# Two node blocks a slot, and twelve passes a layer, for a graph layer's one-hot gathers on TensorE

## The chip, the core and the metric

The kernel runs on one core of a Trainium2 chip. The metric is device time in microseconds (us). The engines are called by their names here and by their short names in the profile: TensorE (PE, its weight loads PEld), VectorE (DVE), ScalarE (ACT), GpSimd (POOL), SyncE (SP). ACTq and SPq are rows of DMAs that ScalarE and SyncE issue.

## The reference, cut to what matters

Two layers of a graph transformer over N = 3125 nodes of D = 128 features and E = 103125 edges that are sorted by their destination; H = 8 heads of 16.

```python
h = relu(layernorm(x0))                          # x0 is the input
for l in range(2):
    xn = layernorm(h) * g1 + b1
    xp = xn + xn @ Wpos + bpos + deg * Wdeg + bdeg   # deg: normalised degree of a node
    q, k, v = (xp @ Wq + bq), (xp @ Wk + bk), (xp @ Wv + bv)
    att   = clip(sum_per_head(q[dst] * k[src]) / 4, -50, 50)
    ex    = exp(att)                             # the softmax's shift cancels
    aggr  = segment_sum(v[src] * ex, dst) / segment_sum(ex, dst)
    h = h + aggr @ Wo + bo
    h = h + gelu(layernorm(h) @ W1 + b1) @ W2 + b2
return x0 + h
```

The edges are the given ones and one self loop per node. What costs time is k[src] and v[src]: a row of 256 floats (1 KB) per edge, from a table of 3200 rows.

## The kernel before, in words

**Tiles and groups.** The edges are 806 tiles of 128 (one edge per partition), handled in groups of 4 tiles: 202 groups a layer, 404 in all (`GROUPS`). The nodes are 25 blocks of 128 (`BLOCKS`). The first 6 groups of a layer are "seam" groups, whose tiles reach over two node blocks and cost two one-hots instead of one. Node blocks are sorted by how soon their edges end, in 9 chunks of 2 or 3 blocks (`CHUNKS`); when all edges of a chunk are summed, its dense work (output projection, norms, feed-forward, the next layer's q, k, v) is laid over the following 21 slots. From the slot of group 31 on some chunk is always in that state.

**A slot** is one turn of the unrolled loop that each engine runs; the engines are tied by semaphores only. In slot n:
- GpSimd (L908 to L920) runs ahead by up to `RING` = 8 groups. It issues one indirect DMA per tile, which gathers 128 rows of 1 KB from the table in HBM into `kvr`.
- TensorE runs `edge_q(n+1)` (L1190: query rows per edge as one-hot times q, 8 matmul records), `edge_sum(n-1)` (L1202: one-hot times messages, 8 records), one `pick` if one is due (L1214), then dense parts. `edge_q(n+1)` waits for VectorE's product of group n, since bank 2 is a single buffer, and for ScalarE's `onehotT`.
- VectorE runs `edge_iteration(n)` (L1891): the product (L1854), the messages of group n-1 (L1878), the sum per head (L1859), clip and guard (L1864, L1869), four additions to `agg` (L1889), the one-hot of group n+2 (L1840); then dense parts.
- ScalarE runs the two exponentials of group n (L1456, L1459), `edge_spread(n+2)` (L1414, L1418, which makes `onehotT`), one `pick_hots` if one is due (L1420), then dense parts.
- SyncE loads `relT` for ScalarE, row by row the one tile in each of 11 groups (`ROW_GROUPS`) that GpSimd does not gather, and stores tables and outputs.

**Picks.** In 7 groups a layer (`PICK_GROUPS` = 36, 63, ... 198) two of the four tiles (`PICKS` = 2) are not gathered by GpSimd but by TensorE, as a product of a one-hot with the whole table. One pass goes over the 25 node blocks, one a slot. For a block, ScalarE issues the DMA of its 128 KB of the table into `pick_kv` (L1433), and makes the one-hot for 256 edges in two operations, |src - node| and relu(1 - ...), each 128x256 (L1438, L1440). TensorE multiplies (L1224, four records a block, 128x256) and accumulates in `picked` (bank 7). Two buffers of `pick_kv` and `pick_hot` alternate. `pick_keep` (L1445) copies the result into `kvr`. So GpSimd issues 806 - 11 - 14 = 781 gathers a layer.

**Prologue.** Blocks are ranked, degrees counted, and the first table is computed. SyncE's order is: bias rows (L695), 14 copies of source rows into `pick_table` (L701), `rel_table` and `relT` (L704, L716), the first `pick_src` (L725), 11 copies into `row_src` (L730), the 13 stores of the first table (L739), the copies of q and x into rank order (L746, L751). GpSimd's first gather waits for the 13 stores.

The lines that say it:

```python
PICK_GROUPS = [36 + 27 * i for i in range(7)]                       # L176
PICK_AHEAD = BLOCKS + 3
        return gathers(n) - by_rows(n) - PICKS * by_pick(n)         # pool_gathers
                if n >= RING:
                    pool.wait_ge(s_msg, n - RING + 1)               # L917
                if n:
                    pe.wait_ge(s_prod, n)                           # L1195, edge_q
                pe.wait_ge(s_msg, n + 1)                            # L1204, edge_sum
```

## Time and profile before

| | |
|---|---|
| runs | 2130.23 us median of three (2128.7 to 2131.04) |
| the profiled execution | 2131.35 us; its span 2129.6 us |
| busy share of the span | PE 73%, PEld 62%, DVE 80%, ACT 58%, POOL 71% |
| granted TensorE clock, mean | 0.917 of full speed |
| chain that ended last | POOL 56%, issue 21%, DVE 8%, DMA 5%, PE 5% |
| costliest groups, us busy | POOL gathers L920 1480; PE L1198 529, L1211 518, L1224 385; DVE L1889 471, L1840 283 |
| DMA | 334 MB in all, mean 157 GB/s; from ScalarE's queue (q10) 47.6 MB |

A busy share is a mean over the whole span. The times of matmul records overlap, since they are pipelined: what one step costs is read from start to start in the timeline. The same holds of VectorE's and ScalarE's rows, where one instruction's record overlaps the next by some 0.1 us. "issue" is time in which an engine waited for nothing that the profile shows.

### The profile page before, as it was taken

The page shows a single profiled execution, that of the slowest core. Times are in us where ns is not written, and L with a number is a line of the kernel's source. Part 1 is how long each engine was busy: PE and PEld are TensorE (multiplying, and loading weights), DVE is VectorE, ACT ScalarE, POOL GpSimd, SP SyncE. Part 2 cuts the span into 40 slices and gives each one's busy share as a digit, 9 for nine tenths or more (in the row PEclk, how much of TensorE's full clock was granted, in tenths as well). Part 3 has the DMA queues.
Part 4 walks back from the last instruction along what each step waited for, and adds up shares of the span by engine and source line. Part 5 has one row for each costly group of instructions (what it writes and reads, how often), then busy time and mean ns, then how long its engine had stood idle before and what let it go on. Part 6 is the DMA issues. An engine that isn't in the chain of part 4 may idle for free.

```text
span 2129.6 us, 45086 instructions
## 1 busy us (share of the span) xinstructions
PE 1561.9 (73%) x9627; PEld 1317.3 (62%) x9627; DVE 1694.2 (80%) x4743; ACT 1232.0 (58%) x2893; POOL 1520.4 (71%) x1620
## 2 busy tenths in 40 slices
PE   4867678787777687777876777767677777777776
PEld 3656566666666566666656666656566666666565
DVE  8759788888888888888877778777787877787775
ACT  8325566575757565665654446556564656456564
POOL 7077777777777777777727777777777777777773
PEclk9979989899999999999988889999998999899998
DMA  2365555555555555555525555555555555555551
GB/s 89 110 190 164 180 175 169 177 174 170 157 167 162 173 160 167 161 163 170 156 71 164 164 163 160 161 158 169 166 157 161 164 169 152 167 163 166 155 159 51
DMA packets 179620, 334.20 MB, mean 157 GB/s; under 512 B 39730, under 2 KB 114684, under 8 KB 179356
## 3 DMA queue, kind: packets, MB, share of 16 engines
q0 software_dynamic: 75424, 205.75, 34.3%
q1 hardware_dynamic: 51660, 77.96, 11.1%
q10 hardware_dynamic: 52272, 47.60, 7.5%
q8 instruction: 88, 1.44, 0.3%
q14 instruction: 176, 1.44, 0.2%
HBM read 319.48 MB, written 8.39 MB: 154 GB/s over the span
## 4 chain that ended last, share of the span: by engine, by line
POOL 56%; issue 21%; DVE 8%; DMA 5%; PE 5%; ACT 3%; SPq 1%; DVEq 0%; ACTq 0%; POOLq 0%
POOL kvr L920 56%; DMA kvr<-kv_table,srcidx 5%; DVE agg L1889 2%; DVE kvr L1495 2%; PE bank L1198 1%; PE bank L1211 1%; DVE msg L1878 1%; ACT L1373 1%; DVE prod L1854 1%; ACT apart L1414 0%; DVE onehot L1840 0%; ACT L1456 0%; PE bank L1155 0%; ACT onehotT L1418 0%; SPq L730 0%
## 5 line engine op out<-in xcount | busy, mean ns | idle before, releaser
L920 POOL DMA_INDIRECT kvr<-kv_table,srcidx x1562 | 1480.1, 948 | 541.7 <-issue 465.7
L1198 PE MATMUL bank<-q,onehotT 128*128 x3320 | 528.7, 309 | 503.8 <-DVE prod L1854 300.7
L1198 PEld LDWEIGHTS bank<-q,onehotT 128*128 128x128 f32 x3320 | 454.6, 212 | 637.7 <-issue 633.0
L1456 ACT ACTIVATE bank<-attc 128x32 f32<-128x32 f32 x404 | 81.2, 201 | 794.0 <-DVE attc L1869 787.5
L1211 PE MATMUL bank<-msg,onehot 128*128 128x136 f32 x3320 | 517.7, 306 | 0.6 <-DVE msg L1878 0.6
L1889 DVE TENSOR_TENSOR agg<-agg,bank 128x136 f32 x1624 | 471.4, 290 | 55.6 <-PE bank L1211 32.1
L1854 DVE TENSOR_TENSOR prod<-kvr,bank 128x512 f32<-128x512 f32 (+1 forms) x404 | 273.5, 677 | 279.2 <-DMA kvr<-kv_table,srcidx 244.2
L1211 PEld LDWEIGHTS bank<-msg,onehot 128*128 128x128 f32 x3320 | 479.1, 216 | 2.3 <-DVE msg L1878 2.2
L1224 PE MATMUL bank<-pick_kv,pick_hot 128*128 128x256 f32 x1400 | 384.9, 399 | 13.8 <-DMA pick_kv<-kv_table 12.6
L1414 ACT ACTIVATE apart<-relT,minus_p 128x512 bf16<-128x512 bf16 x416 | 293.9, 706 | 5.3 <-DMA relT<-rel_table 4.9
L1878 DVE TENSOR_TENSOR msg<-kvr,bank 128x512 f32<-128x512 f32 (+1 forms) x404 | 271.6, 672 | 25.2 <-ACT bank L1456 24.9
L1224 PEld LDWEIGHTS bank<-pick_kv,pick_hot 128*128 128x128 f32 x1400 | 256.9, 203 | 43.7 <-issue 20.5
L1840 DVE TENSOR_TENSOR onehot<-bank,rel 128x512 f32<-128x512 f32 x416 | 283.1, 683 | 0.2
L1859 DVE TENSOR_REDUCE att<-prod 128x32 f32<-128x512 f32 x404 | 273.7, 677 | 0.1
L1418 ACT ACTIVATE onehotT<-apart 128x512 f32<-128x512 bf16 x416 | 261.9, 630 | 13.1
L1438 ACT ACTIVATE pick_apart<-pick_src,minus_node 128x256 bf16<-128x256 f32 x350 | 172.4, 493 | 0.2
L1440 ACT ACTIVATE pick_hot<-pick_apart 128x256 f32<-128x256 bf16 x350 | 145.9, 417 | 11.1
L1459 ACT ACTIVATE msg<-attc 128x32 f32<-128x32 f32 x404 | 85.9, 213 | 0.0
L1864 DVE TENSOR_SCALAR attc<-att 128x32 f32<-128x32 f32 x404 | 79.0, 196 | 0.1
L1869 DVE SCALAR_TENSOR_TENSOR attc<-att,attc 128x32 f32<-128x32 f32 x404 | 75.3, 187 | 0.0
L1456 ACT ACT_TABLE_LOAD x54 | 69.3, 1283 | 1.0
L1155 PE MATMUL bank<-w,hT 128*128 128x128 f32 x400 | 57.9, 288 | 0.0
(223 smaller groups left out, 973.3 us busy)
## 6 DMA issues: line engine op xcount, KB each, us to landing
relT<-rel_table SPq DMA_DIRECT2D x104, 512.0 KB
kv_rows<-kv_table SPq DMA_DIRECT2D x2816, 1.0 KB
pick_kv<-kv_table ACTq DMA_DIRECT2D x350, 128.0 KB
kvr<-kv_table,srcidx POOLq DMA_INDIRECT x1562
loop_kv<-kv_table SPq DMA_DIRECT2D x25, 128.0 KB
kv_table<-qkv SPq DMA_DIRECT2D x25, 128.0 KB
kv_table<-onehot SPq DMA_DIRECT2D x8, 256.0 KB, 2.7
w<-weights SPq DMA_DIRECT2D x2, 840.0 KB, 7.3
```

Source lines behind the costliest of these rows:

```text
L920: pool.indirect_dma_start(kvr[:, n % RING, j, :], None, kv_table[l], bass.IndirectOffsetOnAxis(ap=srcidx[:, step:step + 1], axis=0)).then_ ...
L1198: mm = pe.matmul(bank[2][:, j * D:(j + 1) * D], onehotT[:, m % OHT, j, :], q[:, bass.ds(ranks[j + h], 1), :].rearrange("p a c -> p (a c)") ...
L1211: mm = pe.matmul(sum_ps(n, k), onehot[:, m % OH, j, :], msg[:, n % 2, j, :], start=(m, j) == of[0], stop=(m, j) == of[-1])
L1224: mm = pe.matmul(picked[:, j * KV:(j + 1) * KV], pick_hot[:, m % 2, j * P:(j + 1) * P], pick_kv[:, m % 2, :], start=b == 0 and j == 0, sto ...
L1414: act.activation(apart[:], relT[:, m // BODY % REL_BUFS, r, :], ACT.Abs, bias=minus_p[:]).then_inc(s_apart, 1)
L1418: act.activation(onehotT[:, m % OHT, :, :].rearrange("p j e -> p (j e)"), apart[:], ACT.Relu, bias=1.0, scale=-1.0).then_inc(s_ohT, 1)
L1438: act.activation(pick_apart[:], pick_src[:], ACT.Abs, bias=minus_node[:, b:b + 1]).then_inc(s_pick_apart, 1)
L1840: dve.tensor_tensor(onehot[:, m % OH, :, :], iota_ps.unsqueeze(1).broadcast_to([P, G, P]), rel[:, row:row + G].unsqueeze(2).broadcast_to([ ...
L1854: dve.tensor_tensor(prod[:, 0:t, :], kvr[:, n % RING, 0:t, 0:D], bank[2][:, 0:t * D].rearrange("p (j c) -> p j c", c=D), ALU.mult).then_in ...
L1859: dve.tensor_reduce(att[:, n % 2, 0:t * H], prod[:, 0:t, :].rearrange("p j (h d) -> p (j h) d", d=HD), AX, ALU.add).then_inc(s_att, 1)
L1878: dve.tensor_tensor(by_head(msg[:, n % 2, 0:t, 0:D]), by_head(kvr[:, n % RING, 0:t, D:KV]), ex[:, 0:t * H].rearrange("p (j h) -> p j h", h ...
L1889: dve.tensor_tensor(target, target, sum_ps(n, j), ALU.add).then_inc(s_agg, 1)
```

## The change

- `PICK_GROUPS` has 12 groups a layer (24, 39, ... 189) in place of 7. GpSimd issues 806 - 11 - 24 = 771 gathers a layer.
- A pass takes 13 slots (`PICK_STEPS`): 12 with two node blocks and one with the last. One DMA brings both blocks (256 KB), eight matmul records multiply them.
- ScalarE makes the one-hot of the first block of a slot, with its two operations as before. VectorE makes that of the second, at the end of its `edge_iteration`, with one `tensor_scalar` (is_equal, 128x256 float32, compared with a per-partition scalar of `node`).
- The buffers of the picks move into `x_nat` for layer 0 and into `loops` for layer 1. The first `pick_src` of each layer is loaded by SyncE, behind the x copies and behind the last use of `loops`. The loads of x0 also wait for the last pick of layer 0.
- In the prologue the copies into `pick_table` (now 24) and into `row_src` (11) are issued by ScalarE, behind the square root of the degrees, and no longer by SyncE ahead of the table's stores. SyncE waits for both before it copies q.
- `ROW_GROUPS` begins with 23 in place of 24.

```diff
-ROW_GROUPS = [24 + 17 * i for i in range(11)]
+ROW_GROUPS = [23] + [41 + 17 * i for i in range(10)]
-PICK_GROUPS = [36 + 27 * i for i in range(7)]
+PICK_GROUPS = [24 + 15 * i for i in range(12)]
 PICKS = 2
-PICK_AHEAD = BLOCKS + 3
+PICK_STEPS = -(-BLOCKS // 2)
+PICK_AHEAD = PICK_STEPS + 3
...
@@ SyncE
-            sp.wait_ge(s_rows_f, 2)
-            for i, g in enumerate(PICK_GROUPS):
...
-            sp.wait_ge(s_pick_table, 16 * PICKS * len(PICK_GROUPS))
-            sp.dma_start(pick_src[:], pick_table[0:1, :].broadcast_to([P, PICKS * P])).then_inc(s_pick_src, 16)
-
-            sp.wait_ge(s_rows, 16 * 2 * SC)
-            for i, g in enumerate(ROW_GROUPS):
...
             sp.wait_ge(s_row_src, 16 * len(ROW_GROUPS))
+            sp.wait_ge(s_pick_table, 16 * PICKS * len(PICK_GROUPS))
@@ TensorE, pick(k, t)
+                pe.wait_ge(s_pick_kv[m % 2], 16 * (m // 2 + 1))
+                for h in range(min(2, BLOCKS - 2 * t)):
+                    b = 2 * t + h
+                    if h == 0:
+                        pe.wait_ge(s_pick_hot_act, k * PICK_STEPS + t + 1)
+                    else:
+                        pe.wait_ge(s_pick_hot_dve, k * (BLOCKS // 2) + t + 1)
+                    for j in range(PICKS):
+                        mm = pe.matmul(picked[:, j * KV:(j + 1) * KV], pick_hot[l][:, m % 2, h, j * P:(j + 1) * P], pick_kv[l][:, m % 2, h, :], start=b == 0 and j == 0, stop=b == BLOCKS - 1 and j == PICKS - 1)
@@ ScalarE
             act.activation(degstd[:], degsum_ps, ACT.Sqrt, scale=1.0 / (N - 1)).then_inc(s_degstd, 1)
+            act.wait_ge(s_rows_f, 2)
+            for i, g in enumerate(PICK_GROUPS):
+                for j in range(PICKS):
...
+                    act.dma_start(pick_table[i:i + 1, j * P:(j + 1) * P], step_src_f[row:row + 1, c * P:(c + 1) * P]).then_inc(s_pick_table, 16)
+            act.wait_ge(s_rows, 16 * 2 * SC)
+            for i, g in enumerate(ROW_GROUPS):
...
+                act.dma_start(row_src[i % ROW_PARTS:i % ROW_PARTS + 1, i // ROW_PARTS, :], step_src[row:row + 1, c * P:(c + 1) * P]).then_inc(s_row_src, 16)
@@ ScalarE, pick_hots(k, t)
+                act.dma_start(pick_kv[l][:, m % 2, 0:nb, :], kv_table[l].rearrange("(b p) c -> p b c", p=P)[:, b:b + nb, :]).then_inc(s_pick_kv[m % 2], 16)
@@ VectorE
+            def pick_hots(k, t):
+
+                l, m, b = k // len(PICK_GROUPS), k * PICK_STEPS + t, 2 * t + 1
+                if t == 0:
+                    dve.wait_ge(*pick_src_loaded(k))
+                if m >= 2:
+                    dve.wait_ge(s_picked, m - 1)
+                dve.tensor_scalar(pick_hot[l][:, m % 2, 1, :], pick_src[l], node[:, b:b + 1], None, ALU.is_equal).then_inc(s_pick_hot_dve, 1)
...
                         edge_iteration(n)
+                        k, t = pick_at(n)
+                        if k is not None and 2 * t + 1 < BLOCKS:
+                            pick_hots(k, t)
```

## Rows read from the trace of the kernel before

**Rows 1.** GpSimd's gathers by line, the first gather of layer 0, GpSimd's wait for the ring.

```profile
L920 POOL DMA_INDIRECT kvr<-kv_table,srcidx x1562 | 1480.1, 948 | 541.7 <-issue 465.7 <-DMA kv_table<-qkv 38.6 <-DMA kv_table<-xn 27.7
103.70 0.99 POOL kvr L920
POOL kvr L920 <- DVE msg L1878: 9.8, 32, 0.3
```

**Rows 2.** Windows: us, busy us (instructions) by engine, granted clock, DMA share, GB/s.

```profile
200.00:600.00 400.00, 309.05 (x1850) 260.61 (x1851) 347.42 (x1001) 245.57 (x562) 303.06 (x319) 0.92 0.58 172
600.00:1050.00 450.00, 336.00 (x2054) 282.69 (x2053) 370.16 (x1068) 277.74 (x618) 340.26 (x361) 0.93 0.56 164
1200.00:2050.00 850.00, 623.05 (x3793) 529.66 (x3792) 660.82 (x1875) 491.43 (x1123) 643.04 (x680) 0.93 0.55 162
```

**Rows 3.** VectorE's waits for gathers: in 120:1090, in 300:500, in 1120:2098.

```profile
DVE prod L1854 <- DMA kvr<-kv_table,srcidx: 79.2, 62, 3.4
...
DVE prod L1854 <- DMA kvr<-kv_table,srcidx: 4.6, 7, 1.4
...
DVE prod L1854 <- DMA kvr<-kv_table,srcidx: 165.0, 116, 4.4
```

**Rows 4.** Timeline of VectorE: first and last product of layer 0.

```profile
127.11 0.69 DVE L1854 TENSOR_TENSOR prod<-kvr,bank 128x512 f32<-128x512 f32 x1 [7.99 <-issue]
...
1092.80 0.42 DVE L1854 TENSOR_TENSOR prod<-kvr,bank 128x256 f32<-128x256 f32 x1
```

**Rows 5.** Timelines: two neighbouring products on VectorE; one slot of TensorE.

```profile
460.77 0.68 DVE L1854 TENSOR_TENSOR prod<-kvr,bank 128x512 f32<-128x512 f32 x1
...
464.31 0.68 DVE L1854 TENSOR_TENSOR prod<-kvr,bank 128x512 f32<-128x512 f32 x1
...
462.65 1.15 PE L1198 MATMUL bank<-q,onehotT 128*128 x8 [0.48 <-ACT onehotT L1418]
...
464.56 1.03 PE L1224 MATMUL bank<-pick_kv,pick_hot 128*128 128x256 f32 x4
465.52 0.33 PE L935 MATMUL bank<-bias,ones 3*128 3x384 bf16 x1
```

**Rows 6.** The chain of work: one slot of TensorE at the lower clock.

```profile
393.53 2.07 PE bank L1198 x8
395.60 1.81 PE bank L1211 x8
397.41 1.71 PE bank L1224 x4
```

**Rows 7.** VectorE operations near the new one: timelines, then two lines' durations.

```profile
82.20 0.87 DVE L1654 SCALAR_TENSOR_TENSOR onehot<-u_deg,deg,bank 128x256 f32<-128x256 f32 x2
...
455.86 0.86 DVE L1701 TENSOR_SCALAR xn<-x,mv,rstd 128x128 f32<-128x128 f32 x3
...
L1701 DVE TENSOR_SCALAR xn<-x,mv,rstd x75: 329/345/557, 298.2 to 2117.6; 128x128 f32<-128x128 f32 x75
...
L1584 DVE TENSOR_SCALAR w<-w x2: 220/249/278, 23.3 to 23.9; 128x128 f32<-128x128 f32 x2
```

**Rows 8.** DMA queue q10, that of ScalarE; TensorE's wait for the picks' loads.

```profile
q10 hardware_dynamic: 52272, 47.60, 7.5%
...
PE bank L1224 <- DMA pick_kv<-kv_table: 12.6, 21, 2.1
```

**Rows 9.** Timelines of the prologue: SyncE's DMA issues, VectorE's last product for the table.

```profile
73.53 4.24 SPq L701 DMA_DIRECT2D pick_table<-onehotT  x14
...
82.88 8.23 SPq L730 DMA_DIRECT2D row_src<-q  x11
...
98.56 0.71 SPq L739 DMA_DIRECT2D kv_table<-xn  x1
100.51 19.12 SPq L746 DMA_DIRECT2D q<-qkv  x25
...
94.27 0.48 DVE L1654 SCALAR_TENSOR_TENSOR xn<-u_deg,deg,bank 128x256 f32<-128x256 f32 x1
```

More of the change, by code:

```diff
@@ L387, in build @@
         kv_rows = sb("kv_rows", [P, 2, KV])
-        pick_src = sb("pick_src", [P, PICKS * P])
-        pick_kv = sb("pick_kv", [P, 2, KV])
-        pick_apart = sb("pick_apart", [P, PICKS * P], BF16)
-        pick_hot = sb("pick_hot", [P, 2, PICKS * P])
+        node = sb("node", [P, BLOCKS])
         minus_node = sb("minus_node", [P, BLOCKS])
@@ L450, in build @@
         x0 = x_nat
+        spare = [t[:].rearrange("p b c -> p (b c)") for t in (x_nat, loops)]
+        pick_src = [t[:, 0:PICKS * P] for t in spare]
+        pick_kv = [t[:, 2 * P:2 * P + 4 * KV].rearrange("p (u h c) -> p u h c", u=2, h=2) for t in spare]
+        pick_hot = [t[:, 2 * P + 4 * KV:2 * P + 8 * KV].rearrange("p (u h c) -> p u h c", u=2, h=2) for t in spare]
+        pick_apart = [t[:, 2 * P + 8 * KV:3 * P + 8 * KV].bitcast(BF16) for t in spare]
         spare = q[:].rearrange("p b c -> p (b c)")
@@ L572, in build @@
         s_pick_apart = sem("s_pick_apart")
-        s_pick_hot = sem("s_pick_hot")
+        s_pick_hot_act = sem("s_pick_hot_act")
+        s_pick_hot_dve = sem("s_pick_hot_dve")
+        s_pick_first = sem("s_pick_first")
         s_picked = sem("s_picked")
@@ L695, in _ @@
                 sp.dma_start(bias3[k:k + 1, :, :], bias_parts[k * L * RC:(k + 1) * L * RC, :].rearrange("c (a e) -> c a e", a=1)).then_inc(s_bias3, 16)
-            sp.wait_ge(s_rows_f, 2)
-            for i, g in enumerate(PICK_GROUPS):
-                for j in range(PICKS):
-                    c, row = divmod(row_of(g, at_begin=True) + G - PICKS + j, P)
-                    sp.dma_start(pick_table[i:i + 1, j * P:(j + 1) * P], step_src_f[row:row + 1, c * P:(c + 1) * P]).then_inc(s_pick_table, 16)
             sp.wait_ge(s_rel_bf, 1)
@@ L722, in _ @@
                 rel_rows(body)
-            sp.wait_ge(s_pick_table, 16 * PICKS * len(PICK_GROUPS))
-            sp.dma_start(pick_src[:], pick_table[0:1, :].broadcast_to([P, PICKS * P])).then_inc(s_pick_src, 16)
-            sp.wait_ge(s_rows, 16 * 2 * SC)
-            for i, g in enumerate(ROW_GROUPS):
-                c, row = divmod(row_of(g, at_begin=True) + ROW_TILE, P)
-                sp.dma_start(row_src[i % ROW_PARTS:i % ROW_PARTS + 1, i // ROW_PARTS, :], step_src[row:row + 1, c * P:(c + 1) * P]).then_inc(s_row_src, 16)
             table = kv_table[0].rearrange("(b p) c -> p b c", p=P)
@@ L751, in _, with first_pick_src @@
                     sp.dma_start(x[:, bass.ds(r, 1), :], x_nat[:, b0 + j:b0 + j + 1, :]).then_inc(s_x_ranked, 16)
+            def first_pick_src(l):
+                if l == 0:
+                    sp.wait_ge(s_x_ranked, 16 * BLOCKS)
+                else:
+                    sp.wait_ge(s_looped, NCH)
+                sp.dma_start(pick_src[l], pick_table[0:1, :].broadcast_to([P, PICKS * P])).then_inc(s_pick_first, 16)
+            first_pick_src(0)
             def load_loops(c):
@@ L1212, in edge_sum, with pick @@
                 mm.then_inc(s_agg_ps, 1)
-            def pick(k, b):
-                m = k * BLOCKS + b
-                if b == 0 and k:
+            def pick(k, t):
+                l, m = k // len(PICK_GROUPS), k * PICK_STEPS + t
+                if t == 0 and k:
                     pe.wait_ge(s_pick_kept, k)
-                if b == 0 and k % len(PICK_GROUPS) == 0:
-                    pe.wait_ge(s_agg, sums_by(k // len(PICK_GROUPS) * GROUPS + SEAM_GROUPS))
-                pe.wait_ge(s_pick_hot, m + 1)
+                if t == 0 and k % len(PICK_GROUPS) == 0:
+                    pe.wait_ge(s_agg, sums_by(l * GROUPS + SEAM_GROUPS))
                 pe.wait_ge(s_pick_kv[m % 2], 16 * (m // 2 + 1))
-                for j in range(PICKS):
-                    mm = pe.matmul(picked[:, j * KV:(j + 1) * KV], pick_hot[:, m % 2, j * P:(j + 1) * P], pick_kv[:, m % 2, :], start=b == 0 and j == 0, stop=b == BLOCKS - 1 and j == PICKS - 1)
+                for h in range(min(2, BLOCKS - 2 * t)):
+                    b = 2 * t + h
+                    if h == 0:
+                        pe.wait_ge(s_pick_hot_act, k * PICK_STEPS + t + 1)
+                    else:
+                        pe.wait_ge(s_pick_hot_dve, k * (BLOCKS // 2) + t + 1)
+                    for j in range(PICKS):
+                        mm = pe.matmul(picked[:, j * KV:(j + 1) * KV], pick_hot[l][:, m % 2, h, j * P:(j + 1) * P], pick_kv[l][:, m % 2, h, :], start=b == 0 and j == 0, stop=b == BLOCKS - 1 and j == PICKS - 1)
                 mm.then_inc(s_picked, 1)
```

41 lines of the change are left out of this document (23 added, 18 removed).

## The prediction, made blind

> **What bounds the kernel.** I read the chain of waits first: more than three quarters of it is GpSimd's gathers and the "issue" time between them. The groups by line give the step: 1480.1 us busy and 465.7 us of issue in 1562 gathers, 1.25 us each, and in all only 9.8 us of waiting for a free place in the ring [rows 1]. So GpSimd walks at a constant pace through both layers, 781 x 1.25 = 976 us in each, or 4.83 us a group (976 / 202), and the other engines only have to keep up. How nearly they do is the question of this case. The windows show VectorE busy 87% in the first part of layer 0, 82% in its second part, 78% in layer 1, and TensorE 77%, 75% and 73% [rows 2]. VectorE's waits for gathers are its true spare time: 165 us in layer 1, 79.2 in layer 0, and only 4.6 us between 300 and 500 [rows 3]. There the chain of VectorE, TensorE and ScalarE already fills GpSimd's pace.
>
> **Fewer gathers.** 20 x 1.25 = 25.0 us off GpSimd, 12.5 a layer, if it stays the one that sets the pace. Its pace becomes 771 x 1.25 / 202 = 4.77 us a group.
>
> **The prologue.** SyncE spends 4.24 us on 14 copies into pick_table and 8.23 us on 11 into row_src ahead of the table's stores. The last store goes out at 98.56, though VectorE finished the data at 94.27 + 0.48 = 94.75 [rows 9]. With the copies gone the stores follow VectorE, whose products come 0.8 us apart or slower, and SyncE's issue of one takes 0.7. So the last leaves at about 94.85 and GpSimd begins 3.7 us earlier than 103.70 [rows 1, 9]. ScalarE's new queue: 24 issues of 0.30 and 11 of 0.75, 15.5 us, taken at SyncE's price since no row has them from ScalarE. It was idle there until its first edge spreads, and their results are needed only when q is in place. But SyncE's copies of q, which began at 100.51 [rows 9], wait for those row copies. They could begin when the stores are out, near 95.6, or as late as before: 0 to 4.9 us are won. I take 1.6, nearer the lower end, because ScalarE can start its 15.5 us only after the degrees' root. So the first product, at 127.11 [rows 4], comes at 125.5. Should the 35 issues cost double, it comes 15.5 us later than that, and this falls on layer 0.
>
> **VectorE's new operation.** 12 x 12 x 2 = 288 of them, 144 a layer. No row has this form. The nearest is a scalar_tensor_tensor of 256 columns with a per-partition scalar: two take 0.87 us and one 0.48, so a step of 0.39 [rows 7, 9]. The tensor_scalar of 128 columns with such scalars has a step of (0.86 - 0.345) / 2 = 0.26 [rows 7]. A product of 512 columns takes 0.68 and one of 256 takes 0.42 [rows 4, 5], 0.13 for 128 columns, and 0.26 + 0.13 is the same 0.39. Bounds: 0.33 if the added columns went at double rate, 0.48 if it never overlapped its neighbour, 9 us less or 12 more in a layer. I take 0.395: 56.9 us a layer. A bare VectorE slot grows from 464.31 - 460.77 = 3.54 us [rows 5] to 3.94.
>
> **TensorE's second block.** One block costs 465.52 - 464.56 = 0.96 us, and the slot without dense parts 465.52 - 462.65 = 2.87; with two blocks it is 3.83 [rows 5]. At the lower clock (1.2 of 2.4 GHz) the same slot takes 2.07 + 1.81 + 1.71 = 5.6 [rows 6] and would take 7.3. On average TensorE was busy 309 us in 400, 3.73 a group of 4.83 [rows 2]. Blocks per group rise from 25/27 to 25/15, which adds 0.74 x 0.96 = 0.71: 4.44 of 4.77, 93%. VectorE comes to 347.4 / 400 x 4.83 + 0.395 x 12/15 = 4.51, 95%. Two engines at such shares, tied one slot apart by edge_q's wait for the product, hold each other up: the dense slots of TensorE (feed-forward) are others than those of VectorE (norms, scores). What this costs VectorE per hot slot is in no row. From below it is 0: TensorE's longer stretches of work leave fewer gaps, and the clock, which the windows show at 0.92 to 0.93 with gaps, may be granted in full more often. From above it is 0.96 - 0.395 = 0.56, TensorE's added work pacing every slot. I take 0.15, near the lower end, since a bare slot of 3.83 still fits under 3.94: 21.6 us a layer.
>
> **ScalarE and the queues.** ScalarE makes 312 one-hots in place of 350 and ten more copies of `picked`: no more work than before, and it is not on the path. The loads of picks carry 600 blocks in place of 350. That queue's 7.5% of sixteen engines is 160 us, 0.46 for one load of 128 KB, so 0.91 for a double one, and TensorE was already late for 21 of 350 by 12.6 us [rows 8]. I count nothing extra: edge_q of the next slot has about a microsecond before VectorE needs it. If that cover is gone, 0.46 in each of 288 slots is inside the 0.56 above. The other added waits (s_pick_hot_dve before the next pick_src, VectorE's wait for `picked` of two steps before, SyncE's for x and `loops`) all ask for things finished a slot or more earlier, and what stands behind them on SyncE has slots in hand.
>
> **The sum.** Layer 0, between first and last product: 1092.80 - 127.11 = 965.7 [rows 4], less 79.2 of waiting for gathers, is 886.5 us that the chain of engines itself needs. With the change: 886.5 + 56.9 + 21.6 = 965.0, and the last product comes at 125.5 + 965.0 = 1090.5, 2.3 us earlier than before. GpSimd alone would allow 1092.8 - 3.7 - 12.5 = 1076.6. So I expect layer 0 to be set by the VectorE and TensorE chain, with GpSimd waiting for its ring, and most of its 12.5 us lost. Layer 1 has 165 us of spare against 56.9 + 21.6 + 12.5, so it keeps 12.5 us. Together 14.8 us: 2131.35 - 14.8 = 2116.5 for a profiled execution. That one stands 1.1 us over the median of the three runs, so the median would be 2115.4. I say 2115.
>
> **Rivals.**
> - *Everything is kept* (chance 0.27). If the hold-up per hot slot stays below (1076.6 - 125.5 - 886.5 - 56.9) / 144 = 0.05 us, GpSimd paces both layers. The ring of 8 groups, some 38 us, would bridge the tight stretch from 300 to 500. Time: 2130.2 - 3.7 - 25.0 = 2101.5. For it: the clock could rise. Against it: the two shares of 93 and 95%.
> - *TensorE becomes the bound* (0.15). From a hold-up of (14.8 + 21.6) / 144 = 0.25 us per hot slot on, the kernel is slower than before. At 0.40 layer 0 ends 33.7 us after the old time (36.0 more than at 0.15, less 2.3), layer 1 still keeps its 12.5, since 56.9 + 57.6 + 12.5 is under 165: 2151. For it: one slot at the lower clock needs 7.3 us, over one and a half of GpSimd's groups, and double loads may come late. Against it: such stretches should get rarer.
> - *VectorE's new operation stops GpSimd* (0.04). Then each of 288 gathers that it meets is held for up to its own 0.39 us, 112 us: 2130 - 15 + 112 = 2227. The rows speak against it: the tensor_scalar on L1701 lies between gathers too, takes 329 ns at least and 345 in the middle [rows 7], and GpSimd's step stays 1.25 [rows 1]. The one on L1584, with an immediate as its scalar, takes 220 to 249, less by about what 64 to 128 columns cost, so only the form with an immediate seems to run at double rate, and the new one has a per-partition scalar. The Trainium skill has the rule that speaks for it: VectorE: DVE Perf Modes, "The perf-mode tier table", gives fp32 tensor_scalar double rate from SBUF, and SBUF — State Buffer, "Who interferes with whom", says that an operation in such a two-port mode locks GpSimd out for its whole length.
> - *The prologue gives nothing and the rest little* (0.07): the 35 issues are slow on ScalarE, layer 0 starts late, and the time comes within a few microseconds of before, 2128.
>
> My own case, the partial gain, has 0.47. The range of 8 in 10 goes from 2100, just under the full gain, to 2132, a hold-up of 0.26 us. Faster or slower counts from 0.2%, 4.3 us, which is about what a measurement of this kernel can tell from no change. Faster 0.75: my case and the full gain, with a little of the last rival. Same 0.09: most of the last rival and the near edge of the second. Slower 0.16: the rest.
>
> **What would show it.** In the profile after: 1542 gathers at 1.25 us, the first near 100 us. GpSimd's wait for the messages (its ring), 9.8 us before, grows to some tens of us, all in layer 0; in layer 1 it stays small. VectorE's wait for gathers in layer 0 shrinks from 79 us to near 10, that in layer 1 to about 80. L1224's successor has 2400 records. The new VectorE group has 288 instructions with durations of 0.4 to 0.5 us. TensorE is busy near 85% with a granted clock over 0.93. If GpSimd's ring wait stays under 10 us, the full gain is right. If VectorE waits for TensorE (agg for bank, prod for bank) by more than 60 us, the second rival is. If gathers have a step over 1.25, the third.

## The result, and the profile after

The changed kernel takes 2100.49 us (median of four runs, 2098.28 to 2102.06); the kernel before, on the same chip, 2130.64 (2128.7 to 2131.25). The ratio is 0.9856, with a 95% interval of 0.9844 to 0.9867: 30.1 us, or 1.4%, faster. The forecast was 2115. The case that came true is the first rival, everything kept, at 2101.5; that it lies within 1 us is in part luck (see below). The profiled execution took 2100.35 us with a span of 2098.6, and the differences below are of its span, 31.0 us.

The page of the kernel after: the first line, GpSimd's gathers by line, the chain of waits, ScalarE's DMA queue.

```profile
PE 1715.5 (82%) x10627; PEld 1468.3 (70%) x10627; DVE 1770.0 (84%) x5031; ACT 1206.7 (58%) x2827; POOL 1506.9 (72%) x1601
...
L925 POOL DMA_INDIRECT kvr<-kv_table,srcidx x1542 | 1466.4, 951 | 526.4 <-issue 459.3
...
POOL 34%; issue 19%; DVE 19%; PE 12%; DMA 8%; ACT 6%; DVEq 1%; SPq 0%; ACTq 0%
...
q10 hardware_dynamic: 85360, 81.57, 12.8%
```

1542 gathers, 20 fewer, at the old step: (1466.4 + 459.3) / 1542 = 1.249 us. TensorE went from 73 to 82% of the span and VectorE from 80 to 84%. The chain that ended last runs less through GpSimd (34%, before 56%) and more through VectorE and TensorE, but that chain is one path traced back and not a measure of who holds whom. The wait for the ring is.

Waits of the kernel after: GpSimd's and TensorE's in the whole span, then VectorE's in 120:1085 (layer 0) and in 1100:2078 (layer 1). Columns: us in total, times, longest.

```profile
POOL kvr L925 <- DVE msg L1898: 10.1, 33, 0.3
...
PE bank L1234 <- DMA x_nat<-kv_table: 27.6, 39, 2.4
...
PE bank L1234 <- DMA loops<-kv_table: 25.7, 39, 3.4
...
DVE prod L1874 <- DMA kvr<-kv_table,srcidx: 17.9, 11, 4.7
DVE agg L1909 <- PE bank L1216: 16.5, 35, 2.0
DVE prod L1874 <- PE bank L1203: 16.5, 17, 8.0
DVE msg L1898 <- ACT bank L1476: 15.9, 13, 2.1
...
DVE prod L1874 <- DMA kvr<-kv_table,srcidx: 115.7, 89, 4.5
```

GpSimd waits 10.1 us for its ring, as before (9.8, [rows 1]): nothing holds it, in either layer. TensorE waits 53.3 us for the picks' loads where it waited 12.6 [rows 8], and that does not reach GpSimd's pace either.

Windows of the kernel after, the same stretches as [rows 2], and the columns of them.

```profile
200.00:600.00 400.00, 343.28 (x2120) 295.18 (x2119) 368.72 (x1081) 243.72 (x556) 302.92 (x319) 0.97 0.64 193
600.00:1050.00 450.00, 381.87 (x2359) 326.58 (x2358) 400.42 (x1171) 276.47 (x614) 341.01 (x358) 0.97 0.61 183
...
1200.00:2050.00 850.00, 702.99 (x4330) 607.55 (x4328) 708.66 (x2046) 487.83 (x1111) 643.48 (x678) 0.96 0.60 181
```

In the first window VectorE is 92% busy and TensorE 86%, and GpSimd still issues its gathers at the old pace. The granted clock rose from 0.92 and 0.93 to 0.97 and 0.96: TensorE, fuller now, ran more of its time at the upper of its two levels, 2.4 GHz.

Timelines of the kernel after: the first gather and the last of layer 0, the first of layer 1; the first and last product of layer 0; ScalarE's new DMA issues and SyncE's copies of q; one slot of TensorE with two node blocks.

```profile
100.31 1.00 POOL L925 DMA_INDIRECT kvr<-kv_table,srcidx  x1 [23.29 <-DMA kv_table<-xn]
1068.53 0.95 POOL L925 DMA_INDIRECT kvr<-kv_table,srcidx  x1 [0.30 <-issue]
1103.18 0.94 POOL L925 DMA_INDIRECT kvr<-kv_table,srcidx  x1 [33.70 <-DMA kv_table<-qkv]
...
127.77 0.69 DVE L1874 TENSOR_TENSOR prod<-kvr,bank 128x512 f32<-128x512 f32 x1 [8.04 <-PE bank L1203]
...
1075.59 0.42 DVE L1874 TENSOR_TENSOR prod<-kvr,bank 128x256 f32<-128x256 f32 x1
...
82.72 0.17 ACT L1344 ACTIVATE degstd<-bank 128x1 f32<-128x1 f32 x1 [0.93 <-PE bank L1080]
82.73 7.58 ACTq L1349 DMA_DIRECT2D pick_table<-onehotT  x24
90.36 7.21 ACTq L1353 DMA_DIRECT2D row_src<-q  x11
...
100.47 19.90 SPq L738 DMA_DIRECT2D q<-qkv  x25
...
455.27 1.15 PE L1203 MATMUL bank<-q,onehotT 128*128 x8 [0.89 <-ACT onehotT L1437]
456.26 1.09 PE L1216 MATMUL bank<-msg,onehot 128*128 128x136 f32 x8
457.38 1.97 PE L1234 MATMUL bank<-x_nat 128*128 128x256 f32 x8
```

With the same marks read from both traces (before: first gathers at 103.70 and 1120.46, last ones at 1080.94 and 2096.85; after: last one at 2068.87), the 31.0 us divide so:

| stretch | before | after | gain |
|---|---|---|---|
| to the first gather | 103.7 | 100.3 | 3.4 |
| gathers of layer 0, first to last | 977.2 | 968.2 | 9.0 |
| last gather to last product, layer 0 | 11.9 | 7.1 | 4.8 |
| last product to the first gather of layer 1 | 27.7 | 27.6 | 0.1 |
| gathers of layer 1 | 976.4 | 965.7 | 10.7 |
| last gather to last product, layer 1 | 7.4 | 4.5 | 3.0 |
| last product to the end | 25.3 | 25.2 | 0.1 |

(The rounded gains add to 31.1.) So both layers kept their gain, and each also ended with VectorE closer behind GpSimd. I had forecast nothing of the kind.

### The profile page after: what moved, and what is told of

Read it like the earlier page. It is cut to its first block, busy times and chain, and to the rows that moved or that the text cites. A ratio compares the mean times of both kernels' runs of the same rounds, so it can differ in the third digit from the quotient of the medians.

```text
span 2098.6 us, 47279 instructions
## 1 busy us (share of the span) xinstructions
PE 1715.5 (82%) x10627; PEld 1468.3 (70%) x10627; DVE 1770.0 (84%) x5031; ACT 1206.7 (58%) x2827; POOL 1506.9 (72%) x1601
## 3 DMA queue, kind: packets, MB, share of 16 engines
q1 hardware_dynamic: 51424, 78.08, 11.1%
## 4 chain that ended last, share of the span: by engine, by line
POOL 34%; issue 19%; DVE 19%; PE 12%; DMA 8%; ACT 6%; DVEq 1%; SPq 0%; ACTq 0%
POOL kvr L925 34%; DVE agg L1909 6%; DMA kvr<-kv_table,srcidx 4%; DMA x_nat<-kv_table 3%; PE bank L1203 3%; PE bank L1234 3%; PE bank L1216 3%; DVE kvr L1515 2%; DVE onehot L1860 2%; DVE prod L1874 1%; ACT apart L1433 1%; DVE msg L1898 1%; DVEq L672 1%; ACT L1476 1%; PE bank L1160 1%
## 5 line engine op out<-in xcount | busy, mean ns | idle before, releaser
L925 POOL DMA_INDIRECT kvr<-kv_table,srcidx x1542 | 1466.4, 951 | 526.4 <-issue 459.3
L1203 PE MATMUL bank<-q,onehotT 128*128 x3320 | 494.4, 296 | 274.2 <-DVE prod L1874 134.0
L1909 DVE TENSOR_TENSOR agg<-agg,bank 128x136 f32 x1624 | 472.2, 291 | 50.8 <-PE bank L1216 26.6
L1216 PE MATMUL bank<-msg,onehot 128*128 128x136 f32 x3320 | 486.6, 293 | 1.0 <-DVE msg L1898 0.8
L1216 PEld LDWEIGHTS bank<-msg,onehot 128*128 128x128 f32 x3320 | 448.0, 204 | 3.0 <-DVE msg L1898 2.8
L1234 PE MATMUL bank<-loops 128*128 128x256 f32 x1200 | 296.4, 390 | 29.2 <-DMA loops<-kv_table 25.7
L1234 PE MATMUL bank<-x_nat 128*128 128x256 f32 x1200 | 294.1, 387 | 31.6 <-DMA x_nat<-kv_table 27.6
L1433 ACT ACTIVATE apart<-relT,minus_p 128x512 bf16<-128x512 bf16 x416 | 294.0, 707 | 15.2 <-issue 14.8
L1234 PEld LDWEIGHTS bank<-loops 128*128 128x128 f32 x1200 | 219.2, 193 | 67.1 <-DMA loops<-kv_table 36.7
L1234 PEld LDWEIGHTS bank<-x_nat 128*128 128x128 f32 x1200 | 217.1, 191 | 68.6 <-DMA x_nat<-kv_table 39.3
L1479 ACT ACTIVATE msg<-attc 128x32 f32<-128x32 f32 x404 | 85.9, 213 | 0.0
L1458 ACT ACTIVATE loops<-loops,minus_node 128x256 bf16<-128x256 f32 x156 | 76.9, 493 | 2.7 <-PE bank L1234 2.6
L1458 ACT ACTIVATE x_nat<-x_nat,minus_node 128x256 bf16<-128x256 f32 x156 | 76.8, 492 | 0.0
```

Source lines behind the costliest of these rows:

```text
L925: pool.indirect_dma_start(kvr[:, n % RING, j, :], None, kv_table[l], bass.IndirectOffsetOnAxis(ap=srcidx[:, step:step + 1], axis=0)).then_ ...
L1203: mm = pe.matmul(bank[2][:, j * D:(j + 1) * D], onehotT[:, m % OHT, j, :], q[:, bass.ds(ranks[j + h], 1), :].rearrange("p a c -> p (a c)") ...
L1216: mm = pe.matmul(sum_ps(n, k), onehot[:, m % OH, j, :], msg[:, n % 2, j, :], start=(m, j) == of[0], stop=(m, j) == of[-1])
L1234: mm = pe.matmul(picked[:, j * KV:(j + 1) * KV], pick_hot[l][:, m % 2, h, j * P:(j + 1) * P], pick_kv[l][:, m % 2, h, :], start=b == 0 and ...
L1433: act.activation(apart[:], relT[:, m // BODY % REL_BUFS, r, :], ACT.Abs, bias=minus_p[:]).then_inc(s_apart, 1)
L1458: act.activation(pick_apart[l], pick_src[l], ACT.Abs, bias=minus_node[:, b:b + 1]).then_inc(s_pick_apart, 1)
```

## The experiments

Two accounts stood against each other first. **A**: GpSimd's pace sets both layers, so the gain is that of the gathers, and the engines behind it have room. **B**: much of the gain comes from elsewhere than the gathers (the clock, the rearranged work). Where an expectation names another, it says what that holds. Ratios are to the kernel before, run on the same chip.

**Seven passes.** The changed kernel with the old number of passes, at groups 24 to 186.

```diff
-PICK_GROUPS = [24 + 15 * i for i in range(12)]
+PICK_GROUPS = [24 + 27 * i for i in range(7)]
```

> Two blocks a slot, one-hots and prologue as in the changed kernel, but 7 passes a layer: 781 gathers a layer in place of 771. Theory A (GpSimd's gathers pace both layers, the rest only follows): 20 gathers more at 1.25 us, so 2100.5 + 25 = about 2125, and VectorE's wait for gathers in layer 0 grows from 18 us to over 60. Theory B (the gain came from the slots being packed otherwise and from the fuller clock): less than 12 us over the changed kernel, under 2112.

2121.21 us, ratio 0.9951 (0.9934 to 0.9969). The five passes a layer are worth 20.7 us. That is more than B allows (under 12), and near A's 25; VectorE's wait for gathers in layer 0 is 61.9 us, as A said. In the two profiled executions the gathers of the layers take 24.1 us more with seven passes than with twelve. This kernel's share of the gain, some 9 us, comes without one gather less. 3.6 us are the earlier first gather (100.08), and 7.6 the ends of the layers: the last product trails the last gather by 8.3 and 3.4 us, against 11.9 and 7.4 before. (Its gathers give 4.4 us back, and the way to layer 1's first gather 2.7, in a profiled execution of 2127.07 us, 5.9 over its median.) Both kernels, this one and the kernel before, have seven passes; the last one is now that of group 186 instead of 198 and takes 13 slots instead of 25. Its mean granted clock is 0.888, the lowest of all profiled executions, so the clock is not what pays.

**The prologue undone.** The 35 copies go back to SyncE, ahead of the stores.

```diff
@@ SyncE, ahead of the stores of the first table
+            sp.wait_ge(s_rows_f, 2)
...
+                    sp.dma_start(pick_table[i:i + 1, j * P:(j + 1) * P], step_src_f[row:row + 1, c * P:(c + 1) * P]).then_inc(s_pick_table, 16)
...
+                sp.dma_start(row_src[i % ROW_PARTS:i % ROW_PARTS + 1, i // ROW_PARTS, :], step_src[row:row + 1, c * P:(c + 1) * P]).then_inc(s_row_src, 16)
@@ ScalarE
-            act.wait_ge(s_rows_f, 2)
...
-                    act.dma_start(pick_table[i:i + 1, j * P:(j + 1) * P], step_src_f[row:row + 1, c * P:(c + 1) * P]).then_inc(s_pick_table, 16)
...
-                act.dma_start(row_src[i % ROW_PARTS:i % ROW_PARTS + 1, i // ROW_PARTS, :], step_src[row:row + 1, c * P:(c + 1) * P]).then_inc(s_row_src, 16)
```

> The changed kernel with the copies into pick_table and row_src back on SyncE's queue, ahead of the table's stores. Theory A (GpSimd paces from its first gather on): that gather moves from 100.3 to some us later (with 24 copies in place of 14, to about 106), and the time with it, 2104 to 2107. Theory B (layer 0 is paced by the chain of VectorE and TensorE, whose first product came no earlier in the changed kernel than before): no more than 1 us, unless that first product moves too.

2107.26 us, ratio 0.9888 (0.9873 to 0.9903): 6.8 us lost. Its first gather goes out at 106.91, 6.6 us after the changed kernel's.

```profile
106.91 0.99 POOL L935 DMA_INDIRECT kvr<-kv_table,srcidx  x1 [30.91 <-DMA kv_table<-xn]
```

So 6.6 us at the first gather are 6.8 at the end, about as A said. The first product moved too, but by 4.2 us only (to 131.97), so a layer paced from there would have lost less. It is more than 3.4 because twelve passes need 24 copies where seven needed 14.

**ScalarE makes both one-hots.** VectorE has no new operation.

```diff
@@ ScalarE, pick_hots(k, t)
-                act.activation(pick_apart[l], pick_src[l], ACT.Abs, bias=minus_node[:, b:b + 1]).then_inc(s_pick_apart, 1)
...
-                act.activation(pick_hot[l][:, m % 2, 0, :], pick_apart[l], ACT.Relu, bias=1.0, scale=-1.0).then_inc(s_pick_hot_act, 1)
+                for h in range(nb):
...
+                    act.activation(pick_apart[l], pick_src[l], ACT.Abs, bias=minus_node[:, b + h:b + h + 1]).then_inc(s_pick_apart, 1)
...
+                    act.activation(pick_hot[l][:, m % 2, h, :], pick_apart[l], ACT.Relu, bias=1.0, scale=-1.0).then_inc(s_pick_hot_act, 1)
@@ VectorE
-                        if k is not None and 2 * t + 1 < BLOCKS:
+                        if False:
```

> ScalarE makes both one-hots of a slot, VectorE none. Theory A (VectorE's 144 operations a layer fit into spare time and GpSimd paces): the time stays within 5 us below that of the changed kernel, 2096 to 2101; VectorE's wait for gathers in layer 0 grows from 18 us by about 37. The long gathers (over 970 ns) fall from 73 to near the 18 of the kernel before. Theory C (ScalarE has no room: onehotT comes late): slower, over 2105, with TensorE's wait for onehotT well over 129 us.

2096.6 us, ratio 0.984 (0.9823 to 0.9857): 3.9 us less than the changed kernel. That is inside A's figure, but the intervals of the two ratios overlap, and 2.3 us of it lie ahead of the first gather (98.0 against 100.31), in a stretch that the edit does not touch: kernels with the same prologue have their first gather anywhere from 98.0 to 100.3. Another 2.6 lie in the two layers' gathers. The waits are the finding. VectorE's in 120:1085:

```profile
DVE prod L1873 <- PE bank L1203: 29.3, 22, 8.4
DVE agg L1908 <- PE bank L1216: 27.1, 66, 2.5
DVE msg L1897 <- ACT bank L1475: 22.9, 12, 3.1
DVE rstd L1716 <- ACT std L1258: 17.3, 12, 1.6
...
DVE prod L1873 <- DMA kvr<-kv_table,srcidx: 4.0, 3, 3.3
```

VectorE was relieved of 37 us in layer 0, and its wait for gathers did not grow by that, as A had said: it fell from 17.9 to 4.0, and the waits for TensorE and ScalarE took its place. Under whose name spare time stands depends on which of several inputs comes last. This run does not show that VectorE's being faster is the whole reason, since ScalarE has 132 us more work in each layer and is later for the others: the wait for `std` (17.3) was 0.2 in the changed kernel, and TensorE's for `onehotT` rose from 129.1 to 147.3 in the whole span. The one-hot made twice, below, is the cleaner test.

**The one-hot as tensor_tensor.** The same comparison against a broadcast column.

```diff
-                dve.tensor_scalar(pick_hot[l][:, m % 2, 1, :], pick_src[l], node[:, b:b + 1], None, ALU.is_equal).then_inc(s_pick_hot_dve, 1)
+                dve.tensor_tensor(pick_hot[l][:, m % 2, 1, :], pick_src[l], node[:, b:b + 1].broadcast_to([P, PICKS * P]), ALU.is_equal).then_inc(s_pick_hot_dve, 1)
```

> VectorE's one-hot as tensor_tensor with the node number broadcast, which has two inputs and cannot run at double rate. If the new operation runs at double rate now (step 0.26 us) and stops GpSimd's gathers at times, then the step grows to about 0.33 to 0.40, the long gathers (over 970 ns) fall from 73 to about 20, and the time stays within 3 us of 2100.5, since 10 to 20 us more of VectorE fit into layer 0's spare 18. If the long gathers come from the heavier DMA traffic instead, about 73 stay.

2105.02 us, ratio 0.9877 (0.9855 to 0.9898), 4.5 us slower; the intervals of this ratio and the changed kernel's overlap. The new operation by line (in the changed kernel its mean record is 366 ns):

```profile
L1942 DVE TENSOR_TENSOR x_nat<-x_nat,node 128x256 f32<-128x256 f32 x144 | 60.1, 417 | 4.1 <-PE bank L1234 4.1
```

Start to start it takes 0.33 us, as expected. I had thought that with this form fewer gathers would be stretched, about 20. More were: 90 gathers take over 970 ns, against 73 in the changed kernel, and 69 of the 90 overlap one of these operations in time. The gathers of the two layers take 4.9 us longer (969.8 and 969.0), which is where the time went. The last sections come back to this.

**The one-hot made twice.** VectorE does each new operation a second time into unused space: 144 more operations and 37 us more work a layer.

```diff
+                dve.tensor_scalar(pick_more[l][:, 0, :], pick_src[l], node[:, b:b + 1], None, ALU.is_equal)
                 dve.tensor_scalar(pick_hot[l][:, m % 2, 1, :], pick_src[l], node[:, b:b + 1], None, ALU.is_equal).then_inc(s_pick_hot_dve, 1)
```

> The changed kernel with VectorE's one-hot made twice (the second copy into a place nobody reads): 144 operations a layer more, 0.26 us each, 37 us. Theory A (the chain of VectorE and TensorE had 18 us of spare left in layer 0 and 116 in layer 1, so layer 0 is near its edge): layer 0 grows by about 37 - 18 = 19 us, layer 1 not, 2115 to 2125, and GpSimd starts to wait for its ring. Theory D (there is far more slack than the waits show): under 2106.

2102.65 us, ratio 0.986 (0.9844 to 0.9877): 2.2 us more, less than the changed kernel itself differs between two chips (2103.34 below). The 2115 to 2125 that the wait for gathers alone would give (A) falls, and D holds. Window 600:1050, GpSimd's wait for the ring, and VectorE's waits in 120:1085:

```profile
600.00:1050.00 450.00, 385.43 (x2392) 329.69 (x2393) 422.86 (x1255) 280.47 (x624) 340.88 (x359) 0.98 0.62 184
```

```profile
POOL kvr L926 <- DVE msg L1899: 12.8, 42, 0.3
...
DVE msg L1899 <- ACT bank L1477: 14.6, 13, 2.0
DVE prod L1875 <- PE bank L1204: 14.3, 9, 8.1
DVE agg L1910 <- PE bank L1217: 11.4, 26, 2.5
```

VectorE is 94% busy there and GpSimd waits hardly more than before. The layer's gathers take 967.1 us (968.2 without the second copy). VectorE's wait for gathers, 17.9 us in the changed kernel, is gone, and its waits for TensorE in these two rows fell from 33.0 to 25.7. In all, its idle time between the first and the last product of layer 0 fell from 96 to 62 us, which is nearly what was added. So the spare time is one pool: the added work used up more of it than the 17.9 us that stood under the name of the gathers.

**A third block's work for TensorE.** Two more products a slot, expected to take 0.96 us. The extra ones repeat the first tile of every second block, so the rows picked for that tile hold those blocks three times over.

```diff
-                    for j in range(PICKS):
+                    for j in [0] * PICKS * (h == 1) + list(range(PICKS)):
```

> The changed kernel with TensorE's records of the second block of a slot issued one and a half times to twice (its first tile's product three times in all, so the odd blocks' rows of that tile are added three times): two products more a slot, 0.96 us, 138 us a layer. A hot slot of TensorE becomes 4.79 us without dense parts, above GpSimd's 4.77 a group. Theory A (one extra block cost next to nothing because TensorE still had room, a second one does not fit): clearly slower, 2130 to 2180, with VectorE's waits for TensorE above 100 us. Theory E (TensorE's work hardly matters, the clock gives it back): under 2115.

2129.91 us, ratio 0.9993 (0.9984 to 1.0003): 29.4 us more. E's under 2115 falls; A's 2130 to 2180 is met at its very edge. (Its profiled execution, 2138.46 us, stands 8.5 over its median; the sizes of its stretches are to be read with that.)

Waits in the whole span, and the window of layer 1:

```profile
DVE prod L1874 <- PE bank L1203: 76.0, 72, 8.1
...
DVE agg L1909 <- PE bank L1216: 51.8, 154, 1.4
...
POOL kvr L925 <- DVE msg L1898: 35.4, 57, 2.7
```

```profile
1200.00:2050.00 850.00, 792.54 (x4927) 710.95 (x4927) 712.31 (x2041) 488.88 (x1117) 643.51 (x678) 0.98 0.61 184
```

This is what a bound by TensorE looks like: GpSimd's wait for the ring grows, from 10.1 us to 35.4. VectorE's waits for TensorE grow too, from 54.9 (28.3 and 26.6 in the whole span) to 127.8, but the 60 us that the forecast named as the sign of its second rival is no good line: with both one-hots on ScalarE they are 85.9, in a kernel that isn't slower. The third block costs 17.6 us in layer 0's gathers and 21 at its end (the last product trails the last gather by 26.7 us), and 0.5 in layer 1, where TensorE is 93% busy. Start to start, by the median over the slots, the picks' records take 1.83 us for two blocks and 2.59 for three, so two more products are 0.76 us and not 0.96: 109 us a layer. VectorE had room for 37 us a layer; TensorE had it for 109 in layer 1, and not in layer 0.

**Two useless operations.** ScalarE makes both one-hots, and VectorE runs a 128x128 tensor_scalar, whose result nobody reads, in each slot where the changed kernel has its own, though earlier in the slot, ahead of the guard. Its input is in SBUF in one kernel and in PSUM in the other.

```diff
+                    dve.tensor_scalar(pick_more[l][:, t % 2, 0:P], iota_free[:], node[:, 2 * t + 1:2 * t + 2], None, ALU.is_equal)
```

```diff
+                    dve.tensor_scalar(pick_more[l][:, t % 2, 0:P], iota_ps, node[:, 2 * t + 1:2 * t + 2], None, ALU.is_equal)
```

> ScalarE makes both one-hots, and VectorE gets one operation a slot of no use ahead of its guard: tensor_scalar is_equal, 128 columns, from SBUF to SBUF, with a per-partition scalar. If single-input operations from SBUF to SBUF hold up GpSimd, the long gathers (over 970 ns) rise from the 26 with no such operation to 50 or more. If not, about 26. The time is 2096 to 2102 either way.

> The same as the kernel before it in this series, but the useless operation reads its 128 columns from PSUM. If it is the second SBUF port that matters, the long gathers stay near 26; if any further VectorE operation does it, they rise as with the SBUF one. The time is within 3 us of that one's.

2104.65 us, ratio 0.9867 (0.9851 to 0.9883), and 2104.57, ratio 0.9871 (0.985 to 0.9892): the same time, but above the 2096 to 2102 that I had expected. Operation and gathers by line, the SBUF kernel first:

```profile
L1938 DVE TENSOR_SCALAR x_nat<-iota_free,node 128x128 f32<-128x128 f32 x144 | 44.7, 310 | 0.0
...
L926 POOL DMA_INDIRECT kvr<-kv_table,srcidx x1542 | 1465.5, 950 | 531.5 <-issue 457.7 <-DMA kv_table<-qkv 38.7 <-DMA kv_table<-xn 23.2
```

```profile
L1938 DVE TENSOR_SCALAR x_nat<-bank,node 128x128 f32<-128x128 f32 x144 | 49.0, 340 | 0.0
...
L926 POOL DMA_INDIRECT kvr<-kv_table,srcidx x1542 | 1463.1, 949 | 535.4 <-issue 460.2 <-DMA kv_table<-qkv 42.8 <-DMA kv_table<-xn 23.3
```

The mean gather differs by 1 ns. Counted one by one, 42 gathers take over 970 ns with the SBUF input and 24 with the PSUM one; 26 do with no such operation (ScalarE makes both), 18 in the kernel before. Of the 42, 14 overlap the operation in time; of the 24, none does. So the two engines get in each other's way when the operation's input lies in SBUF, and not when it lies in PSUM, and the effect is small.

What both kernels cost over 2096.6, some 8 us (6 to 7 by the ratios, whose intervals just overlap), lies elsewhere. In the profiled executions the first gather is 1.3 and 2.1 us later, and the last product of layer 0 trails the last gather by 11.1 us with the SBUF input and by 16.2 with the PSUM one, against 7.8. So with both one-hots on ScalarE, VectorE seems to have less room than in the changed kernel, where 37 us more made that lag 8.7 us and not 7.1. These are single executions, and it was not taken apart.

**The changed kernel once more, and thirteen passes.** The second kernel has 13 passes a layer.

```diff
-PICK_GROUPS = [24 + 15 * i for i in range(12)]
+PICK_GROUPS = [24 + 14 * i for i in range(13)]
```

> The changed kernel once more, to stand beside the next three on the same chip: 2100.5 within 2 us.

> The changed kernel with 13 passes a layer, one every 14 groups: 4 gathers fewer, 5 us. Theory A (GpSimd paces, and VectorE still has room, as the doubled one-hot showed): 2095.5, 5 us under the changed kernel. Theory F (TensorE's added work of 24 products a layer, near 12 us, is the nearer edge and lengthens the end of layer 0): no gain, 2099 to 2106.

2103.34 us for the changed kernel, ratio 0.9858 (0.9843 to 0.9873), and 2095.0 for thirteen passes, ratio 0.9818 (0.9805 to 0.9831): 8.3 us less on the same chip, where four gathers fewer account for 5.0. In the two profiled executions, which differ by 6.8 us, the layers' gathers take 3.5 us less and the last products trail by 2.0 less. It has the lowest median of this study, though the interval of its ratio overlaps that of the kernel with both one-hots on ScalarE. VectorE's waits in 120:1085:

```profile
DVE prod L1874 <- PE bank L1203: 16.5, 18, 8.0
DVE msg L1898 <- ACT bank L1476: 15.7, 12, 2.6
DVE agg L1909 <- PE bank L1216: 13.7, 33, 2.3
DVE prod L1874 <- DMA kvr<-kv_table,srcidx: 11.5, 11, 2.1
```

Nothing has grown there: layer 0 still follows GpSimd.

**Both together, and fourteen passes,** with ScalarE making both one-hots.

```diff
-PICK_GROUPS = [24 + 15 * i for i in range(12)]
+PICK_GROUPS = [24 + 14 * i for i in range(13)]
...
+PICK_GROUPS = [24 + 13 * i for i in range(14)]
```

> ScalarE makes both one-hots, 13 passes a layer. Theory A: 5 us under the same with 12 passes, so about 2092. Theory F: no gain over 2096.6, 2095 to 2102.

> ScalarE makes both one-hots, 14 passes a layer, one every 13 groups, so that a pass begins before the last one's result is copied out of its bank. Theory A: 2087. Theory F: TensorE waits for that copy in each pass and has no slot to recover in, 2100 or more.

2098.58 us, ratio 0.9838 (0.9819 to 0.9857), for thirteen. The runs give no sign that the two gains add: they lie from 2095.3 to 2106.6, and in the profiled one (2103.3) layer 0 ends later, its last product trailing by 15.0 us (6.5 in the other kernel of thirteen). 2178.06 us, ratio 1.0211 (1.0198 to 1.0225), for fourteen. Its waits:

```profile
PE bank L1231 <- ACT kvr L1469: 121.1, 26, 9.0
...
POOL kvr L925 <- DVE msg L1897: 70.6, 68, 6.2
```

A pass takes 13 slots and here the next begins at once. TensorE waits 4.7 us, a whole slot, in 26 places for ScalarE's copy of the last `picked`, with its other work queued behind. The bank `picked` is single, and with a gap of one slot between passes (thirteen) the copy is hidden. Fourteen passes with VectorE's half of the one-hots were not tried.

## Why the prediction was wrong

**What it had right.** GpSimd sets the pace; 1542 gathers at 1.25; the first gather 3.7 us earlier (measured 3.4); TensorE 0.96 us a block (two take 1.83 start to start, 0.91 each); the granted clock over 0.93 (0.945); layer 1 with spare left, where VectorE's wait for gathers is 115.7 us, which is 165 less 37.4 for the new operation (144 x 0.26, below) and 12.5, so no hold-up at all. From its last product of layer 0 to the end the gain is 13.8 us against 12.5 forecast. Nearly all of the miss, 14.9 of 16.1 us, is the last product of layer 0: said to come at 1090.5, it came at 1075.59, a microsecond from the 1076.6 that "GpSimd alone would allow".

The sum had the chain of engines in layer 0 need 965.0 us; by the same accounting it needed 929.9 (step 2). Of these 35.1 us too many, 19.5 are step 1 and 15.6 step 2. Against them stand 2.3 us by which the first product came later than forecast, and 17.9 in which VectorE still waited for gathers: 35.1 - 2.3 - 17.9 = 14.9.

**The rival's number was in part luck.** 2101.5 is 3.7 + 25.0 us below the kernel before. Measured are 3.4 and 19.7, and 7.8 at the ends of the layers, which stood in nobody's sum.

**Step 1, the size of VectorE's operation: 0.26 us, not 0.395.** Timeline of VectorE in the changed kernel:

```profile
453.39 0.35 DVE L1942 TENSOR_SCALAR x_nat<-x_nat,node 128x256 f32<-128x256 f32 x1
453.65 0.56 DVE L1814 TENSOR_TENSOR loops<-loop_kv,loops 128x384 f32<-128x384 f32 x1
```

Start to start it is 0.26, below my lower bound of 0.33. The nearest row was the wrong one. I scaled the tensor_scalar of 128 columns up by a product's 0.13 and dismissed the fast rate ("only the form with an immediate seems to run at double rate"). That row, though, takes two scalars and this one takes one; the useless operation with one scalar and 128 columns takes 0.19 us start to start from SBUF (0.26 from PSUM), in the same stretch of its kernel:

```profile
452.60 0.28 DVE L1938 TENSOR_SCALAR x_nat<-iota_free,node 128x128 f32<-128x128 f32 x1
452.79 0.18 DVE L1889 SCALAR_TENSOR_TENSOR attc<-att,attc 128x32 f32<-128x32 f32 x1
```

So 128 further columns cost 0.07 us, half of a product's 0.13, and a scalar per partition does not prevent it. The page I weighed had it right: the Trainium skill, VectorE: DVE Perf Modes, "The perf-mode tier table", gives fp32 tensor_scalar double rate from SBUF, and these 0.07 us against 0.13, and 0.26 for 256 columns against 0.39 for the nearest scalar_tensor_tensor, agree with it. This term alone was 19.4 us a layer too high. With 0.26 in it, my own inequality for the first rival would have read (1076.6 - 125.5 - 886.5 - 37.4) / 144 = 0.19 us a hot slot, and the 0.15 that I assumed passes it: the first rival would have been my forecast.

**Step 2, the hold-up: near 0.04, not 0.15.** By the same accounting after, the layer took 1075.59 - 127.77 = 947.8, less 17.9 of waiting for gathers, 929.9. That is 43.4 more than 886.5: 37.4 for the operation and 6.0 for all else, 0.04 us in each of 144 slots. The shares of 93 and 95% that spoke against the rival came as 86% for TensorE and 92% for VectorE in the first window, and GpSimd's wait for its ring stayed at 4.9 us in layer 0. (Step 3 takes this accounting itself apart; it holds between these two kernels, since their other waits are alike.)

**Step 3, "the chain of engines itself needs 886.5 us": the step in which the method failed.** It took the wait for gathers as the only spare time and all other idle time of VectorE as necessary. Were that so, the one-hot made twice would have raised layer 0 to 929.9 + 37.4 = 967.3 us between its products, 19.5 over the 947.8 of the changed kernel. It took 948.4. VectorE's other idle time, the waits for TensorE above all, shrank when VectorE was later for it, and absorbed what the wait for gathers did not. The two operations a slot are 74.8 us a layer over the kernel before, nearly the 56.9 + 21.6 = 78.5 that my sum added. So even with my too high figures layer 0 would have followed GpSimd, and this step, more than the sizes, is what the forecast failed by. What isn't absorbed is the work of a third block on TensorE.

**The first product** was to come 1.6 us earlier and came 0.7 later (127.77, before 127.11). The copies of q began at 100.47, before 100.51, so nothing was won, one end of my bound: ScalarE began only at 82.73, behind the degrees' root, and issued its last copy at 97.6. The issues were cheaper than taken, 7.58 / 24 = 0.32 and 7.21 / 11 = 0.66 us, 14.8 in all. It did not matter: GpSimd's pace counts from its own first gather, and VectorE caught up with it.

**The second rival** lies one block further: not the changed kernel, but the one with a third block's products. **The third** exists as a mechanism and had the wrong price. One of its stretched gathers in the changed kernel, which begins 0.10 us after VectorE's new operation; GpSimd's timeline, then VectorE's:

```profile
400.01 1.07 POOL L925 DMA_INDIRECT kvr<-kv_table,srcidx  x1 [0.30 <-issue]
```

```profile
399.91 0.35 DVE L1942 TENSOR_SCALAR x_nat<-x_nat,node 128x256 f32<-128x256 f32 x1
```

73 gathers are over 970 ns (18 before), and 46 of them overlap one of the 288 operations. All 46 begin 0.09 to 0.19 us after it. What each takes over the median of 946 ns, 0.07 us on average, and its distance from the operation's start add to 0.21 to 0.22 us every time: it is held until the operation, 0.26 us start to start, is nearly over. The other way round, 44 of the 288 operations have records over 360 ns, up to 582, and all 44 overlap a gather, 36 of them beginning 0.4 to 0.7 us into it. Most operations meet a gather at another moment, and then neither is held.

So the price is 3.1 us for the 46 gathers where the forecast for this rival had 112. With the operation gone (both one-hots on ScalarE) the layers' gathers take 2.6 us less. All gathers together are 5.2 us longer than at the mean of before, which is what the layers' 9.0 and 10.7 us lack of 12.5 each; the other 2 us were not taken apart. The count varies between two executions of the same kernel, 73 and 51, of which 46 and 26 overlap the operation. But the kernels whose VectorE has no such operation with its input in SBUF have 17 to 26 long gathers, and those that have it 42 to 90.

The Trainium skill, SBUF — State Buffer, "Who interferes with whom", has a double-rate operation and GpSimd exclude each other for an instruction's whole length; the trace agrees where the two collide, and shows that they do so only at some moments of a gather. It also lists operations with two SBUF inputs against GpSimd instructions that read SBUF. The gathers read their row numbers from SBUF (`srcidx`), and the tensor_tensor, with two SBUF inputs, held 69 of them by 0.13 us each, 9.3 us in all, so the trace agrees with that too.

**The ends of the layers,** 7.8 us of the gain, stood in no step. Nothing in my sum was the distance from the last gather to the last product, 11.9 and 7.4 us before. The kernel with seven passes shortens it as well (8.3 and 3.4), without fewer gathers, and so does the one with the prologue undone (8.4 and 3.4), so neither is the cause. The earlier and shorter last pass is the likeliest, but no run changes it alone: the cause stays open.

## What to carry to other kernels

Where engines are tied to each other, the idle time of one is a single pool under several names. Don't subtract one wait and call the rest needed; ask instead what would have to be late for the pacing engine to stop, and read that from its own wait (here GpSimd's ring, 10 us before and after). To find the real margin, add useless work to one engine at a time: 37 us a layer on VectorE were free within 2 us; 109 on TensorE were free in layer 1 and cost 29 us in layer 0, whose dense work also makes the next layer's q, k and v. Look at the lag between the pacing engine's last piece and the last use of it at each seam: it counts in full. And leave a slot between two passes that share an accumulator.

## What the hardware showed that was not expected

- A float32 tensor_scalar with one per-partition scalar takes 0.26 us start to start for 256 columns and 0.19 for 128, with its input in SBUF; from PSUM it takes 0.26 for 128. As a tensor_tensor 256 columns take 0.33.
- Such an operation holds a gather of GpSimd (946 ns) that begins 0.09 to 0.19 us after it, by 0.03 to 0.13 us. Long gathers are 73 or 51 of 1542 with it, 90 as a tensor_tensor, 24 with its input in PSUM (and 128 columns), 26 without it. It costs some 3 us in 2100.
- The granted clock rose with TensorE's work, though not in strict order. In 1200:2050 it was 0.93 before, where TensorE was 73% busy, 0.96 after (83%), 0.97 with thirteen passes (85%) and 0.98 with a third block's work (93%); but 0.90 at 75% with seven short passes and 14 slots without picks between them.
- DMA issues on ScalarE cost about what they cost on SyncE: 0.32 us for a piece of `pick_table` (0.30), 0.66 for one of `row_src` (0.75).
